# Two-layer attention and feed-forward kernel: GpSimd issues the transfers that fan k out to its products' rows

## The reference

```python
# layer 0: 16 heads of 16 dims, no mask; beside it a mixture of 8 experts
qkv = (xn @ W_qkv + b_qkv);  scores = softmax(einsum('bhip,bhjp->bhij', q, k));  out = scores @ v
# layer 1: causal attention twice with the same k and v; beside it a low-rank ffn
ctx  = causal_attn(q, k, v)
q2   = conv1d(ctx, conv_w, width 3) + conv_b
ctx2 = causal_attn(q2, k, v);  out = ctx2 @ out_w.T + out_b
```

## Time and profile before

| | us |
|---|---|
| median of 3 runs | 1966.15 (1963.6 to 1976.36) |
| the profiled execution | 1965.93 |
| its span, first to last instruction | 1964.1 |
| PE busy | 1795.0 (91%) |
| DVE busy | 1254.4 (64%) |
| ACT busy | 1023.1 (52%) |
| POOL busy | 338.6 (17%) |

### The profile page before, as it was taken

How to read it: one execution, slowest core, us unless ns; L and a number is a source line. 1 busy time by engine, 2 the same in 40 slices (tenths; PEclk the granted TensorE clock), 3 DMA queues, 4 the chain that set the end, 5 groups by cost and what they waited for, 6 DMA issues and landing times.

```text
span 1964.1 us, 31719 instructions
## 1 busy us (share of the span) xinstructions
PE 1795.0 (91%) x10745; PEld 880.7 (45%) x10745; DVE 1254.4 (64%) x3788; ACT 1023.1 (52%) x2064; POOL 338.6 (17%) x525
## 2 busy tenths in 40 slices
PE   4868999999889999997789898999999999999987
PEld 2313555555344555541234344445554454545443
DVE  6675555555644555557553766778786777777673
ACT  1444565655546555655554344555554555555544
POOL 2222211121111222113443101101010101111000
PEclk7878999999989999998999899999999999999999
DMA  6655432343754443332105243655454455555330
GB/s 160 181 142 139 79 65 75 79 90 73 180 111 74 65 71 60 53 48 78 51 22 80 37 63 50 82 77 82 77 72 72 66 78 75 85 75 74 61 50 23
DMA packets 144654, 155.79 MB, mean 79 GB/s; under 512 B 24696, under 2 KB 131472, under 8 KB 144496
## 3 DMA queue, kind: packets, MB, share of 16 engines
q1 hardware_dynamic: 123584, 114.71, 35.5%
q0 software_dynamic: 9024, 14.42, 4.1%
q10 hardware_dynamic: 11888, 24.64, 3.8%
HBM read 55.93 MB, written 33.69 MB: 46 GB/s over the span
## 4 chain that ended last, share of the span: by engine, by line
PE 68%; DVE 11%; DMA 7%; SPq 5%; issue 4%; ACT 3%; POOL 2%; ACTq 0%; DVEq 0%; POOLq 0%
PE p_PV L1138 12%; PE p_S L1121 9%; PE p_S L1065 5%; PE p_S L1082 5%; SPq L2307 5%; PE p_Ma L1341 4%; DMA t_R<-t_msp 4%; PE p_Ma L1221 4%; PE p_S L1198 4%; DVE p_S L1509 3%; PE p_S L1125 2%; PE p_Ma L1364 2%; PE p_Mb L1198 2%; DVE t_mx L1495 1%; PE p_S L1221 1%
## 5 line engine op out<-in xcount | busy, mean ns | idle before, releaser
L1969 ACT ACTIVATE t_R<-p_S 128x512 f32<-128x512 f32 (+1 forms) x1216 | 682.4, 578 | 552.2 <-PE p_S L1125 396.8
L1509 DVE CUSTOM_DVE_ANT_0 p_S<-p_S,t_NM 128x128 f32<-128x128 f32 x1008 | 474.7, 515 | 201.4 <-PE p_S L1082 198.4
L1121 PE MATMUL p_S<-t_R 99*128 99x512 bf16 (+3 forms) x1536 | 475.2, 333 | 34.6 <-DMA t_R<-t_msp 17.3
L1495 DVE TENSOR_REDUCE t_mx<-p_S 128x1 f32<-128x512 f32 x512 | 347.9, 686 | 242.3 <-PE p_S L1065 240.1
L1138 PE MATMUL p_PV<-t_R 128*17 128x512 f32 (+3 forms) x3072 | 329.8, 502 | 1.2 <-issue 1.0
L1082 PE MATMUL p_S<-t_R 96*128 96x128 bf16 x1008 | 255.3, 305 | 19.1 <-DMA t_R<-t_spl 10.4
L1121 PEld LDWEIGHTS p_S<-t_R 99*128 99x128 bf16 x1536 | 150.9, 98 | 173.4 <-ACT t_R L1969 69.0
L1065 PE MATMUL p_S<-t_R 96*128 96x512 bf16 x512 | 202.1, 397 | 26.6 <-DVE t_mx L1495 16.2
L2171 POOL CAST t_spl<-t_rr 128x512 bf16<-128x512 f32 x80 | 49.5, 619 | 911.1 <-DVE t_rr L1467 911.1
L1125 PE MATMUL p_S<-t_NM 128*128 128x128 bf16 x1024 | 199.4, 220 | 0.0
L1509 DVE DVE_READ_ACCUMULATOR2_ANT t_mx<- 128x1 f32 x1024 | 143.9, 140 | 0.1
(11 more groups left out here) (282 smaller groups left out, 2157.2 us busy)
## 6 DMA issues: line engine op xcount, KB each, us to landing
t_R<-t_spl SPq DMA_DIRECT2D x480, 128.0 KB
t_R<-in_w ACTq DMA_DIRECT2D x32, 512.0 KB, 8.1
t_R<-ks SPq DMA_DIRECT2D x96, 128.0 KB
ks<-t_spl SPq DMA_DIRECT2D x16, 384.0 KB, 5.2
hTd<-t_NM SPq DMA_DIRECT2D x39, 128.0 KB
ysd<-t_NM SPq DMA_DIRECT2D x39, 128.0 KB
t_NM<-hTd SPq DMA_DIRECT2D x39, 128.0 KB, 2.5
ysd<-t_NM POOLq DMA_DIRECT2D x39, 128.0 KB, 3.1
```

Of the source, the lines that this page charges most:

```text
L1121: t = self.nc.tensor.matmul(bank[:, z, :], ka[0:99, h, kb * 128:(kb + 1) * 128], qa[0:99, h, n0:512], start=True, stop=not u.causal)
L1495: nc.vector.tensor_reduce(m.mx[:, g, 4 * j + qb:4 * j + qb + 1], m.S1[s1_bank(k)][:, :], AX.X, ALU.max).then_inc(s.s1_read, 1)
L1509: x = nc.vector.tensor_tensor_reduce(out=sc, in0=sc, in1=m.maskq[:, 512 - n:512], scale=1.0, scalar=NEG, op0=ALU.add, op1=ALU.max, accum_o ...
L1969: nc.scalar.activation(m.P1X[kb][j0 // per] if u.causal else m.P[p % 2][:, j0:j0 + per, :], m.s2_bank(k)[:, 0:per * n].rearrange("p (j n) ...
```

## The change

The six transfers of k are issued by POOL, for every unit of both layers. POOL's `fan` stands right behind `low` of k in kinds 0 and 1, and for kind 2 at the step at which SP had it, which is ahead of `low` of q. Both engines make the same waits for the free buffer. SP keeps the six transfers of q. What is transferred, to where, and the semaphores are the same.

```diff
+def fan_waits(e, s, u):
+    if u.n in (16, 17):
+        e.wait_ge(s.ones_rows, 8)
+    elif u.n == 18:
+        e.wait_ge(s.y2_mm, 2 * NB)
+    elif u.n >= 3:
+        e.wait_ge(s.pv_mm, 8 * (u.n - 2))
...
 class GpSimdE(Engine):
     def project0(self, u, z, i):
         if z < 2:
             self.low(u, z)
+        if z == 1:
+            self.fan(u)
+
+    def fan(self, u):
+        g, e, m, s = self.nc.gpsimd, self.e, self.m, self.s
+        if u.kind < 2:
+            e.wait_ge(s.lo_done, QK[u.n, 1])
+            of = [m.spl[:, 1, p, :] for p in KP]
+        else:
+            e.wait_ge(s.d_ks, 16 * (VN[1, u.b, u.c] - 16))
+            of = [m.ks[2 * u.b + u.c][:, p, :].rearrange("(d h) n -> d h n", h=8) for p in KP]
+        fan_waits(e, s, u)
+        for j, part in enumerate(of):
+            g.dma_start(m.KA[u.buf][16 * j:16 * j + 16, :, :], part).then_inc(s.d_f[1][u.buf], 16)
+
+    def fan1(self, u, z):
+        if z:
+            self.fan(u)
...
 class SyncE(Engine):
     def project0(self, u, z, i):
-        if z < 2:
-            self.fan(u, z)
+        if z == 0:
+            self.fan(u)
...
+    def fan(self, u):
+        e, m, s = self.e, self.m, self.s
+        e.wait_ge(s.lo_done, QK[u.n, 0])
+        fan_waits(e, s, u)
+        for j, p in enumerate(QP):
+            self.start(m.QA[u.buf][16 * j:16 * j + 16, :, :], m.spl[:, 0, p, :], s.d_f[0][u.buf])
```

More of the change, by code:

```diff
@@ L2319, in project0 @@
     def project0(self, u, z, i):
-        if z < 2:
-            self.fan(u, z)
-    def fan(self, u, z):
+        if z == 0:
+            self.fan(u)
+    def fan(self, u):
         e, m, s = self.e, self.m, self.s
[L2326 to L2340, removed]
+        e.wait_ge(s.lo_done, QK[u.n, 0])
+        fan_waits(e, s, u)
+        for j, p in enumerate(QP):
+            self.start(m.QA[u.buf][16 * j:16 * j + 16, :, :], m.spl[:, 0, p, :], s.d_f[0][u.buf])
     def maxp0(self, u):
```

## The result

| | before | after |
|---|---|---|
| median, us (20 runs each) | 1971.86 (1963.6 to 1979.24) | 1974.74 (1972.06 to 1982.29) |
| ratio, 95% interval | | 1.0024 (1.0013 to 1.0036) |
| the profiled execution, us | 1965.93 | 1974.59 |
| its span, us | 1964.1 | 1972.4 |
| POOL busy, us | 338.6 | 493.0 |

A forecast was written before the change was run, and what follows sets the result against it. Anything delaying TensorE was taken as paid in full, its largest wait being for the rows of the maxima. From 1965.93, -16 + 3.3 + 7.0 + 0.7 = -5.0 gave 1961 us, range 1951 to 1990.

The forecast's parts named there:

- Term 1: Layer 1: rows of the maxima wait behind six transfers in place of twelve; -16 us, bounds 0 and 17.1.
- q's six are the only ones ahead: Term 1, unit 26: with k in POOL's queue, only q's six transfers stand ahead of the rows.
- the rows then land near 1345: Term 1, unit 26: rows land near 1345, 2 us before 1347.17, so nearly all their waits go.
- q's landing among k's packets: Term 1, unit 26: sharing engines with k, q's remaining five or so us take up to twice as long, to about 1344.
- the rows come no sooner: Rival, layer 1: two queues share the engines, term 1 is nothing, layer-0 costs stand; 1977 us, chance 0.17.
- k's landing unchanged: Layer 1, unit 26: k still lands at about 1347, set by the engines' data; no change in time.
- k lands late: Rival: POOL issues take 2.1 us each in place of 1.17, so k lands late; about 2011 us, chance 0.18.
- Kind 2: Units of kind 2: POOL's k fan, now ahead of q's `low`, fits into idle time; costed at nothing.
- Term 2: Start of layer 0: the first Newton iteration starts later behind six POOL issues; +3.3 us, bounds 1.5 and 3.3.
- Term 3: Unit 3: third gather stands behind six POOL issues and TensorE waits for it; +7.0 us, bounds 5.2 and 9.
- The other fans of layer 0: Layer 0 beyond units 1 and 3: gathers at unit 5 and the like at unit 7 slightly late; +0.7 us for all.
- better-overlap rival: Two streams beat one: k lands up to 3 us sooner, the first unit's wait shrinks; 1952.5 us, chance 0.15.

The follow-up runs named there:

- layer 1 alone: Against the kernel before, POOL issues k's fans in layer 1 only and SP keeps layer 0's: ratio 0.9999 (0.9984 to 1.0014).
- two of six: Kernel before, all fans by SP, but from unit 18 the last two k transfers of kind 1 units are issued behind the rows: 0.9904 (0.9881 to 0.9927).
- three: Kernel before, all fans by SP, but from unit 18 three k transfers of kind 1 units are issued behind the rows: 0.9977 (0.9957 to 0.9997).
- all three kernels that had it: The change (1.0024), k by POOL in layer 0 only against the kernel before (1.0030), the change with half of k's bytes from unit 20 (0.9924).

## Why the prediction was wrong, point by point

**Term 1 failed, at its step "q's six are the only ones ahead" and "the rows then land near 1345".** Forecast -16 us, measured no gain: waits for the rows 20.1 against 19.5, and 0.9999 with layer 1 alone. The step before it, q's landing among k's packets, was not the trouble: q's last data packet at unit 26 starts 11.3 us after the first issue, where 1344 meant 11.9. But I had the rows land 1 us behind q's data, and they land 2.4 us behind it (1352.49 against 1350.11), 0.5 behind k's (1351.95). I counted the transfers ahead in SP's queue, while the quantity that matters is the bytes issued ahead in all queues, which the change left as they were: k's six go out from 1340.38 to 1343.53, before the rows at 1345.97. The sum of that step was too kind as well. The 5 to 5.5 us that q still had at 1335.1, taking twice as long, end at 1345 to 1346 and not at 1344, which leaves the rows about 1 us of gain or less even by that reasoning. Rows in the prediction pointed the same way: DMA engines 0.92 busy at 143 GB/s, and rows waiting under 0.6 us for the sequencer. One reading was off besides: the chain's 4.70 us run from the start of the third issue, like the median of 1.8, so 2.9 of them are spent behind the fans' data and not 3.5. I gave the rival "the rows come no sooner" 0.17; its mechanism is what happened.

**k's landing unchanged** was right. The two waits for t_spl are 10.2 us as before (10.4), and none came at a unit of kind 1. The rival "k lands late", which needed issues over 1.6 us, fell: they take 0.53 to 0.54. Beside it I had set a rule of the Trainium skill (page "SBUF — State Buffer", section "SBUF: two separate sides"). DVE was busy 12.84 of 14 us around the six issues of 3.15 us at unit 26, and nothing of POOL's was held up. Whether any of DVE's work there takes the shared ports in the way that the page means isn't known, so no run here tests the rule.

**Kind 2** was right in time, no new wait of PE.

**Term 2, mis-sized**: +3.3 forecast, nothing measured. Six issues took 3.21 us from 64.53, not 7.0, and the first iteration starts 3.78 us after the end of `low`, where it was 3.75 (68.01 and 69.52 on the clock of the span; the list runs earlier since the first unit's fans).

```profile
64.53 3.21 POOL L2189 DMA_DIRECT2D t_R<-t_spl  x6 [0.30 <-POOL t_spl L2201]
68.01 0.29 POOL L2126 TENSOR_TENSOR t_nt_<-t_rs 128x4 f32<-128x4 f32 x1 [0.27 <-DVE t_rs L1425]
```

Its input from DVE comes 0.27 us after POOL is free: the issues fit into a wait of 3.75 us that was already in the earlier trace rows. I priced the delay from the end of `low` and did not hold it against that idle time.

**Term 3, right in mechanism, mis-sized**: +7.0 forecast, +4.1 measured (5.00 against 0.89), and 1.4 more by the clock behind the wait, which no term had. The price of an issue was wrong: I took 0.87 us and a gap of 0.30 from the accumulating stores and the gathers, the only other DMAs on POOL. The lower bound, six of 0.87, was too high as well.

**The other fans of layer 0**: +0.7 forecast, none seen. The gather of unit 5 starts at 297.62 (290.13 before), and PE comes to its transposes at 305.58 without a wait; before it was 301.78. The 3.8 us between them stem from unit 3 and are carried along: PE starts on the third gather 2.3 us later than before (183.80 against 181.47; it had come to it 1.8 us earlier) and loses 1.4 more up to the fourth.

**Sum.** With terms 1 and 2 at nothing, term 3 at 4.1, 1.4 by the clock and -1.0 at the first unit the sum is +4.5; the ratio says +4.7 (2.6 to 7.1). The "rows no sooner" rival gave 1977, 11 us up, because it carried my two oversized terms. The better-overlap rival had only that 1.0 us of the first unit's fans, of the 3 that it named, and it comes from issuing in two lists: the data moved no faster, 142 GB/s on two queues, 143 on one.

## What to carry to other kernels

A small transfer waits for the bytes that were issued before it, whoever issued them: moving the big ones to another engine's queue doesn't clear its way, issuing a part of them after it does. How many to put behind is a count between two deadlines, and one more than fits costs most of the gain again (here two of six: -0.96%, three: -0.23%). Before pricing issues that are added to an engine's list, look at the wait that follows them there (free, at the start of layer 0) and for whatever somebody is already late for (unit 3, paid in full, and then some by TensorE's clock), and don't take one DMA's issue time for another kind's.

## What the runs showed of the hardware

POOL's issue of a 128 KB transfer of k's fan took 532 to 544 ns back to back, its accumulating one 882, its gather 977. SP's are slower in this kernel: six of the same size take 3.8 us at most places, and 5.04 at unit 26. The same k data went as packets of another size: data packets of 4096 bytes with POOL, 1024 with SP. With the small ones that raise the semaphores, q0 gained 37.77 MB in 13,824 packets, and on q1 the same transfers had been 41,472. The bytes per second in the fans' stretch were the same (142 and 143) with half of them in the larger packets, so packet size was not what limited them. What does limit them is open: the stretch moves 142 GB/s while a whole transfer of 128 KB goes to only 16 partitions, and no experiment here spread the writes wider.

Over the two queues of the change, transfers were served in the order in which their issues ended, at 13 of 14 places without an exception. A wait of TensorE of 4.8 to 5.0 us at unit 3 was followed by 3.4 to 6.8 us at the lower clock level in all three kernels that had it, and in none of the ten others.
